# A decoder layer on one core: batch 0's mixture-of-experts stage sent through tiles of rows by expert, batch 1's kept dense

## The reference

```python
router_logits = x @ wg.T
probs = softmax(router_logits, axis=-1)
topk_w, topk_idx = top_k(probs, 2)
topk_w = topk_w / sum(topk_w, axis=-1, keepdims=True)
expert_w = sum(one_hot(topk_idx, 8) * topk_w[..., None], axis=1)
h1 = einsum('th,eih->tei', x, w1)      # i = 256 hidden units per expert
h3 = einsum('th,eih->tei', x, w3)
y = einsum('tei,ehi->teh', silu(h1) * h3, w2)
out = einsum('te,teh->th', expert_w, y)
```

## Time and profile before

| | us |
|---|---|
| median of 3 runs | 278.3 (276.68 to 278.51) |
| profiled execution | 279.73 |
| its span, first to last instruction | 278.0 |

### The profile page before, as it was taken

How to read it: one execution, slowest core, us unless ns; L and a number is a source line. 1 busy time by engine, 2 the same in 40 slices (tenths; PEclk the granted TensorE clock), 3 DMA queues, 4 the chain that set the end, 5 groups by cost and what they waited for, 6 DMA issues and landing times.

```text
span 278.0 us, 4261 instructions
## 1 busy us (share of the span) xinstructions
PE 256.4 (92%) x1294; PEld 158.6 (57%) x1294; DVE 189.1 (68%) x577; ACT 159.2 (57%) x298; POOL 121.4 (44%) x183
## 2 busy tenths in 40 slices
PE   7968899989998999999988989999999999999980
PEld 3345665766664755767643747457575565565630
DVE  5457878785999798466554698625989645545573
ACT  1568577776789767878686646684252423332300
POOL 9973191184332443325343420034562754554431
PEclk9968999999999999999999999999999999999995
DMA  7920000020001200000222000000000000000011
GB/s 250 343 81 1 2 0 1 2 63 15 2 0 39 112 4 4 0 0 4 75 75 75 2 1 0 2 1 0 2 0 0 1 2 0 0 0 0 2 38 38
DMA packets 5861, 8.62 MB, mean 31 GB/s; under 512 B 720, under 2 KB 3280, under 8 KB 5712
## 3 DMA queue, kind: packets, MB, share of 16 engines
q1 hardware_dynamic: 5264, 7.57, 8.6%
q10 hardware_dynamic: 576, 0.79, 0.9%
HBM read 7.83 MB, written 0.52 MB: 30 GB/s over the span
## 4 chain that ended last, share of the span: by engine, by line
PE 81%; ACT 8%; DVE 4%; issue 3%; DMA 1%; POOL 1%; POOLq 0%; DVEq 0%; ACTq 0%
PE psA L878 10%; PE psB L907 10%; PE psO L1016 10%; PE psO L930 9%; PE psB L785 4%; PE psJ L814 3%; PE psB L786 3%; PE psB L787 3%; PE psA L786 3%; PE psA L787 2%; PE psA L785 2%; ACT prob L1118 2%; PE psO L935 2%; PE psJ L891 2%; PE psJ L791 2%
## 5 line engine op out<-in xcount | busy, mean ns | idle before, releaser
L1298 DVE CUSTOM_DVE_ANT_0 junk<-psA,c 128x128 bf16<-128x128 f32 (+3 forms) x128 | 56.0, 487 | 15.0 <-PE psA L878 14.5
L756 POOL TENSOR_TENSOR gated<-silu,wbc 128x512 f32<-128x512 f32 x32 | 40.9, 1285 | 42.0 <-DVE hid L1414 21.9
L1118 ACT ACTIVATE prob<-psB 128x512 f32<-128x512 f32 (+1 forms) x88 | 47.5, 560 | 12.4 <-PE psB L907 10.5
L878 PE MATMUL psA<-kst,qa 128*128 128x512 f32 (+1 forms) x88 | 38.4, 451 | 3.3 <-ACT kst L1081 1.8
L907 PE MATMUL psB<-qb,kst 128*128 128x512 f32 (+3 forms) x128 | 38.7, 346 | 1.5 <-DVE kc L1240 0.6
L1172 ACT ACTIVATE silu<-psA 128x512 f32<-128x512 f32 x32 | 19.2, 600 | 35.5 <-PE psA L787 35.1
L1404 DVE SCALAR_TENSOR_TENSOR silu<-silu,psA 128x512 f32<-128x512 f32 x32 | 21.8, 682 | 19.7 <-ACT silu L1172 19.6
L1303 DVE TENSOR_REDUCE negm<-psA 128x3 f32<-128x462 f32 (+1 forms) x48 | 25.8, 579 | 13.0 <-PE psA L878 12.9
L1016 PE MATMUL psO<-hid,w 128*128 128x512 f32 x64 | 32.7, 593 | 0.0
L907 PEld LDWEIGHTS psB<-qb,kst 128*128 128x128 f32 x128 | 22.8, 188 | 16.4 <-issue 7.4
L741 POOL TENSOR_SCALAR_AFFINE_SELECT prob<-prob 128x256 f32<-128x256 f32 x32 | 13.0, 407 | 42.6 <-ACT prob_more L1118 42.6
(11 more groups left out here) (152 smaller groups left out, 504.5 us busy)
## 6 DMA issues: line engine op xcount, KB each, us to landing
c<-w_dram SPq DMA_DIRECT2D x8, 256.0 KB, 2.8
w<-w_dram SPq DMA_DIRECT2D x1, 1024.0 KB, 4.8
c<-c_dram SPq DMA_DIRECT2D x1, 666.0 KB, 7.8
xT<-xt_dram SPq DMA_DIRECT2D x2, 256.0 KB, 5.0
x_tok<-x_dram SPq DMA_DIRECT2D x1, 512.0 KB, 9.0
out_dram<-x_tok SPq DMA_DIRECT2D x2, 256.0 KB, 2.3
wx<-wx_dram SPq DMA_DIRECT2D x1, 384.0 KB, 7.1
c<-c_dram ACTq DMA_DIRECT2D x1, 320.0 KB, 6.4
```

What stands on the lines that cost most here:

```text
L756: nc.gpsimd.tensor_tensor(gated[:, n % 2, :], silu[:, n % 2, :], wbc[:, (E * b + f // 2) % 2, :], ALU.mult).then_inc(s_sg, 1)
L878: last = nc.tensor.matmul(ps[:, c:c + heads * width].rearrange("p (n w) -> p n w", n=heads), qa[:, u % SLOTS, 128 * i:128 * i + 128], keys ...
L1118: nc.scalar.activation(dst, psB[n % SIZE["B"]][:, 0:cols], ACT.Exp, scale=SCALE).then_inc(b_done[n % SIZE["B"]], 1)
L1298: last = nc.vector.tensor_tensor_reduce(out=junk[:, p, cols], in0=psA[p][:, cols], in1=c32[:, C_MASK + S - width:C_MASK + S], scale=-1.0, ...
```

## The change

Batch 0's dense expert stage (F1, F3, F2, BC, WT, YE and YT of batch 0) goes. Instead:

- `RT`: from the two expert numbers of each token VectorE marks choices; TensorE counts, with a triangular and an all-ones matrix, how many tokens before this one chose the same expert; VectorE turns ranks into places in a list in which every expert's tokens fill whole tiles of 128 rows, 15 tiles at most.
- `SX`: eight indexed transfers, issued by GpSimd, write 128 token rows each to their places in a buffer in device memory (`xs_d`). That buffer is zeroed at the start from a cleared key stack.
- `TE`: VectorE works out each tile's expert, and TensorE loads 15 numbers into registers.
- `XL` loads the rows back, four tiles at a time, issued by SyncE; `XS` transposes and splits them.
- `R1`, `R2`, `R3` for each of the 15 tiles: now the tokens are stationary and the weights move, addressed by register; silu and product on 256 hidden units; two transposes; two fp32 matmuls with w2.
- `YD` stores the results two tiles at a time; `YG` fetches them back to their tokens with eight indexed transfers; `YC` weights the two and adds the residual, on VectorE.

The row maxima's split (`MP`) of cross-attention moves from GpSimd to VectorE. The weights w1 and w3 share one buffer `wp`, so that one matmul moves 256 columns of each. Some buffers get other places. Cut to its core:

```diff
+NT = S * 2 // 128 + E - 1
+SEND = 1.2
-        add("MP", (u,), [("POOL", 0.55)], ...
+        add("MP", (u,), [("POOL", 0.55) if st == 0 else ("DVE", 0.4)], ...
+            add("RT", (), [("DVE", 0.55), ("PE", 0.6, 0), ("DVE", 1.7)], [("LG", (0,))])
+    for n in range(2 * QT):
+        add("SX", divmod(n, QT), [("POOL", SEND)], [("RT", ())], after=2.2)
+    add("TE", (), [("DVE", 0.5), ("PE", 1.5)], [("RT", ())])
+    for k in range(-(-NT // 4)):
+        add("XL", (k,), [("SP", 0.6)], [("SX", (1, QT - 1)), ("CQ2", (1,))] + ([(("XS", (k - 2,)), 0)] if k >= 2 else []), after=2.2)
+        add("XS", (k,), [("PE", 0.44), ("ACT", 0.5), ("DVE", 0.6)], [("XL", (k,))],
+            [(1, (("R1", (4 * k - 5,)), 0))] if k >= 2 else [])
+    for t in range(NT):
+        late = [(1, (("R1", (t - 2,)), 2)), (2, (("R2", (t - 2,)), 0))] if t >= 2 else []
+        add("R1", (t,), [("PE", 0.72), ("ACT", 0.32), ("DVE", 0.8)],
+            [("XS", (t // 4,)), ("TE", ()), ("WS", (2 * WC - 1,)), (("SQ", (1, 1, NG - 1)), 0)], late)
+        add("R2", (t,), [("PE", 0.24), ("ACT", 0.32)], [("R1", (t,))], [(1, (("R3", (t - 2,)), 0))] if t >= 2 else [])
+        add("R3", (t,), [("PE", 0.46), ("ACT", 0.22)], [("R2", (t,)), ("W2", ())], [(1, ("YD", (t // 2 - 2,)))] if t >= 4 else [])
+        if t % 2 or t == NT - 1:
+            add("YD", (t // 2,), [("SP", 0.6)], [("R3", (t,))], after=2.2)
+    for n in range(2 * QT):
+        add("YG", divmod(n, QT), [("POOL", SEND)], [("YD", ((NT - 1) // 2,)), last_pv(NU - 1)], after=2.2)
+    add("YC", (), [("DVE", 2.0)], [("YG", (1, QT - 1)), ("GATE", (0,)), ("LNX", (1, 1))])
...
+            sp.wait_ge(s_kz, SLOTS - 1)
+            sp.dma_start(xs_d.rearrange("(p n) d -> p (n d)", p=128),
+                         kst[:, SLOTS - 1, :, :].rearrange("p j t -> p (j t)")[:, 0:NT * D].bitcast(FP32)).then_inc(s_xz, 16)
...
+                    nc.gpsimd.indirect_dma_start(
+                        out=xs_d[:, :], out_offset=bass.IndirectOffsetOnAxis(ap=place_u[:, QT * k + i:QT * k + i + 1], axis=0),
+                        in_=x_tok[:, 0, i, :], in_offset=None).then_inc(s_sx, 16)
...
+                elif kind == "RT":
+                    nc.tensor.matmul(ps[:, 0:E * (QT + 1)], c16[:, H_TRI:H_TRI + 128], flat(chosen[:, :, :]), start=True, stop=False,
+                                     skip_group_check=True)
+                    for i in range(QT):
+                        rest_of = chosen[:, i:i + 1, :].to_broadcast([128, QT - i, E])
+                        last = nc.tensor.matmul(ps[:, E * (i + 1):E * (QT + 1)].rearrange("p (n e) -> p n e", e=E), c16[:, H_ONES:H_ONES + 128],
+                                                rest_of, start=False, stop=i == QT - 1, skip_group_check=True)
+                elif kind == "TE":
+                    pe.wait_ge(s_te, 1)
+                    for t in range(NT):
+                        expert_at.append(pe.value_load(tile_u[0:1, t:t + 1], min_val=0, max_val=I * (E - 1)))
+                elif kind == "R1":
+                    w = [wp[:, :, p, bass.ds(expert_at[t], I)] for p in range(PAIR)]
+                    nc.tensor.matmul(ps, xr_high[:, t % 8, :], w[0], start=True, stop=False)
+                    nc.tensor.matmul(ps, xr_low[:, t % 8, :], w[0], start=False, stop=False)
+                    nc.tensor.matmul(ps, xr_high[:, t % 8, :], w[1], start=False, stop=True).then_inc(s_a, 1)
+                elif kind == "R3":
+                    for n in range(2):
+                        at = I * (t % 2) + 128 * n
+                        last = nc.tensor.matmul(ps[:, 0:128], hT[:, at:at + 128], w2[:, bass.ds(expert_at[t] + 128 * n, 128)],
+                                                start=n == 0, stop=n == 1)
...
+                elif kind == "YC":
+                    for k in range(2):
+                        for i in range(QT):
+                            ins = nc.vector.scalar_tensor_tensor(out=z[:, i, :], in0=back[:, k, i, :], scalar=gsm[:, 0, 4 + k, i:i + 1],
+                                                                 in1=x_tok[:, 0, i, :] if k == 0 else z[:, i, :], op0=ALU.mult, op1=ALU.add)
```

More of the change, by code:

```diff
@@ L319, in schedule @@
             key = what if isinstance(what[0], tuple) else last(what)
-            extra = table[key[0]][2] if key == last(key[0]) else 0.0
+            extra = 0.0 if isinstance(what[0], tuple) else table[key[0]][2]
             before[item, n].append((key, LATENCY[table[key[0]][0][key[1]][0]] + extra))
@@ L484, in layer_kernel @@
         ot_sb = sb("ot_sb", [128, S])
-        junk = sb("junk", [128, SIZE["A"], S], BF16)
+        junk = shared("junk", [128, SIZE["A"], S], BF16)
+        choice = sb("choice", [128, 2, QT, E])
+        chosen = sb("chosen", [128, QT + 1, E], BF16)
+        over = sb("over", [128, E, E * QT])
+        first_tile = sb("first_tile", [128, E])
+        place = sb("place", [128, QT, E])
+        place_f = sb("place_f", [128, 2 * QT])
+        place_u = sb("place_u", [128, 2 * QT], U32)
+        before_t = sb("before_t", [1, 16, E - 1])
+        tile_f = sb("tile_f", [1, 16])
+        tile_u = sb("tile_u", [1, 16], U32)
+        sb("unused", [128, 232])
+        xs = rest
+        back = prob[:, 0, 0:2 * S].rearrange("p (k i d) -> p k i d", k=2, i=QT)
         z = sb("z", [128, QT, D])
@@ L561, in layer_kernel @@
         s_xh = sem("s_xh")
+        s_rt = sem("s_rt")
+        s_pl = sem("s_pl")
+        s_te = sem("s_te")
+        s_xz = sem("s_xz")
+        s_sx = sem("s_sx")
+        s_xl = [sem("s_xl0"), sem("s_xl1")]
+        s_rh = sem("s_rh")
+        s_rth = sem("s_rth")
+        s_ht = sem("s_ht")
+        s_yd = [sem("s_yd0"), sem("s_yd1")]
+        s_yg = sem("s_yg")
         s_sg = sem("s_sg")
@@ L603, in stack_free @@
                 eng.wait_ge(s_kz, u)
+                if u == SLOTS - 1:
+                    eng.wait_ge(s_xz, 16)
             else:
@@ L1242, in _ @@
                     free(JOB[item], last)
+                elif kind == "MP":
+                    u, = args
+                    p = u % 2
+                    fill_done(dve, "A", [("A", (u, k)) for k in range(len(a_fills(u)))])
+                    job_filled(dve, ("MT", (u - 2,)))
+                    rows = mpad[:, p, :, :].rearrange("q i (j c) -> q i j c", c=32)
+                    link(nc.vector.tensor_copy(rows[:, :, :, ROWS], negm[:, p, :, :]))
+                    nc.vector.tensor_tensor(rows[:, :, :, ROWS + 1], negm[:, p, :, :], rows[:, :, :, ROWS].bitcast(FP32),
+                                            ALU.subtract).then_inc(s_mp, 1)
                 elif kind == "VH":
@@ L1451, in constants @@
     c32[:, C_POW:C_POW + QT] = -0.5
+    first = np.full((E, E, QT), BIG, f)
+    for e in range(E):
+        first[e, :e] = 128 * np.arange(QT)
+    c32[:, C_THR:C_TAU] = first.reshape(-1)
+    c32[:, C_TAU:C_TAU + 16] = np.arange(16)
     c16 = np.zeros((128, NC16), f)
+    c16[:, H_TRI:H_TRI + 128] = np.arange(128)[:, None] < np.arange(128)
+    c16[:, H_ONES:H_ONES + 128] = 1
     c16[:, H_ID:H_ID + 128] = np.eye(128)
```

329 lines of the change are left out of this document (239 added, 90 removed), and 3 rows, old and new, of the table RINGS.

## The result

The changed kernel takes 282.9 us (median of 4 runs, 282.64 to 285.21) against 278.3 before (4 runs): a ratio of 1.020, 95% interval 1.013 to 1.026. It is slower, by 1.3 to 2.6%, where 275 and a gain of 1% had been forecast. The profiled execution has a span of 281.0 us, 3.0 more than before.

A forecast was written before the change was run, and what follows sets the result against it. TensorE was taken as the bound. First routed product at 195.5, plus 67.0 of TensorE work, 1.5 for VectorE, 2.3 for the clock, gives 266.3; with the 8.75 tail, span 275.0, forecast 275, range 266 to 286.

The forecast's parts named there:

- TensorE's relief of some 14 us: On TensorE 41 us of batch 0's dense work go; 25 us plus RT and TE come.
- The scatters: Eight on GpSimd from about 178, 1.2 us each, 9.6 in all, to 187.7; landed 190.0, rows loaded back 192.8.
- Rivals 1 and 2: Scatters slow at 2.3 us each, sum 283.8, chance 0.2; or cheap at 0.43 each, 269, chance 0.15.
- rival 1: Scatters at 2.3 instead of 1.2 us each: routed tiles start at 204.3, 284 on the median's scale; chance 0.2.
- TE at 1.5 us: Fifteen register loads on TensorE, at the planner's 1.5 us instead of 6.5 from the nearest row, an issue on a queue.
- Delay batch 1's chain by 5, which the routed tiles mostly cover: 276: Within rival 3: register loads at 6.5 us delay batch 1's chain by 5, mostly covered by routed tiles, time 276.
- Rival 3: Register-addressed matmuls or register loads cost TensorE: end 290 at 0.20 per matmul, 276 with loads at 6.5 us; chance 0.1.
- A tile of 1.56 us: TensorE time per routed tile: R1 0.89, R2 0.22, R3 0.45; 23.4 us for 15 tiles.
- TensorE near idle from 187 to 195, clock falling: Sign of being right: TensorE lacks filler before the routed tiles, 2 us of work in 9; half speed costs 2.3 us.
- Dense work of batch 1 from about 207: After batch 1's transposes near 197.5, router, gates and broadcast take 9.5 us, then its dense tiles begin.
- rival 4: Gathers in GpSimd's queue ahead of gate products make dense tiles wait: two or three 2 us stalls, about 279; chance 0.1.
- The return hidden: YD, gathers, YC and layernorm, 22 us, hidden behind batch 1's dense tiles if the last routed tile is done by about 250.

The follow-up runs named there:

- experiment 6: The kernel with one unchecked load, with every scatter issued twice, the second into a buffer nobody reads: 285.3 us.
- Experiment 4: The changed kernel with one load instruction for all fifteen registers and no bounds checks: 273.2 us, ratio 0.985 to the kernel before.
- experiment 9: One unchecked load, plus maxima split back on GpSimd, batch 0's last normalisation later on VectorE, or both: 272.6, 272.0 and 272.8 us.
- experiment 1: The changed kernel without register loads or register addresses, tile t fixed to expert t // 2: 271.8 us.

## Why the prediction was wrong, point by point

- **TensorE's relief of some 14 us:** right, 14.8.
- **The scatters:** right. The first issue came at 175.1 where 178 was forecast, the period is 1.27 where 1.2 was, so the last ended at 185.2 instead of 187.7, and the first rows were back at about 189.3 instead of 192.8. Rivals 1 and 2 are out; experiment 6 shows that rival 1's mechanism is real: rows that come 10.1 us later cost 12.7 us. The forecast had priced it at one for one (8.8 later, 8.8 longer), without the clock. That its total of 284 for 2.3 each is near the 285.3 measured for 2.5 a pair is luck: it was added to a sum 4 too high. (The terms given for the date of the first routed product add up to 195.0, not to 195.5; nothing hangs on that.) Experiment 4 had 0.6 us of spare, so the kernel stands right at that edge.
- **TE at 1.5 us:** wrong, 9.47 with its stop. This is the mis-sized term. The nearest row, the issue of 0.43, would have given 6.5, and even that is below what came. The number taken was the plan's, with no reason given. That the plan's other costs agree with rows, the ground given for its scatter price, would not have carried it: none of those rows was a register instruction.
- **The page's floor:** the floor of about 600 ns that the Trainium skill (DMA: Bandwidth & Descriptors, Latency and other measured facts) gives a `tensor_load` led to the prediction's estimate of 9 us for TE, and the stop of 9.47, 0.63 a load, is near that. The parts are others: 0.27 for each further load and 0.15 for each of its two checks. At the price so estimated the prediction still added only 1 us, which is the step below.
- **"Delay batch 1's chain by 5, which the routed tiles mostly cover: 276", and 1 us for all of TE at 9:** this step failed, and it did more harm than the size. The routed tiles couldn't cover anything. They stand in the same queue behind the loads, and they need the loaded numbers. The stop went into batch 1's attention, which is the chain that sets the end, and came out whole: 8.20 of 8.20, with 2.50 for the clock on top (the windows of experiment 4). With the 10.2 us by which the kernels with the dear and the cheap TE differ, the same forecast would have said 285. Rival 3 had the right cause at 0.1 and the wrong price.
- **Register-addressed matmuls:** R1 takes 0.49 + 0.23 + 0.25 in the chain (0.50 + 0.23 + 0.25 with fixed addresses), and the kernels with and without addresses differ by 0.7 us in all. The forecast of nothing was right.
- **A tile of 1.56 us:** about right (first R1 0.97, then two transposes 0.22 and R3 0.45), but the tiles of batch 1's waiting time come 1.9 us apart: 15 first products from 202.51 to 228.79. A tile above 1.8 us, and a first one after 202, were named as signs of being wrong, and both showed.
- **TensorE near idle from 187 to 195, clock falling:** it was idle earlier and longer, 178.06 to 187.53, and for another reason. Without the checked loads the forecast hole hardly existed: 8.39 of 9.14 us busy from 179.96 to 189.10 at a clock of 1.00. From 180 to 200 it was idle for 3.6 us there (8.48 and 7.95 busy in the two windows), not for the 8.5 us of filler that went, and the 2.3 us forecast for the clock were not lost. Against that, attention was to end near 186 and ended at 189.1. Why it didn't shorten by its filler is not settled; another plan (half the scatters, replanned) brought it to 187.2.
- **Dense work of batch 1 from about 207:** 224.9, and 214.75 with one unchecked load. From the transposes of batch 1 (L1081, 201.46) to the first dense product it took 13.3 us there, not 9.5. VectorE's routed products stand between the router's small operations, and TensorE's routed tiles ahead of the gates' transposes. But the 13 tiles done by then, against the six or seven that I had counted, made the rest shorter: 56.1 us behind the first dense product, where 275 - 207 = 68 was forecast. The sum of 275 without the stop was thus 4 too high (270.8).
- **The gathers (rival 4):** right to give it little. They fit between the gate products. Timeline of GpSimd, the kernel after:

```profile
240.44 1.29 POOL L868 TENSOR_TENSOR gated<-silu,wbc 128x512 f32<-128x512 f32 x1
241.90 0.99 POOL L859 DMA_INDIRECT prob<-ys_dram,place_u  x1 [0.16 <-DVE hid L1675]
242.90 1.31 POOL L868 TENSOR_TENSOR gated<-silu,wbc 128x512 f32<-128x512 f32 x1
```

- **The return hidden:** not quite. On VectorE the weighting of batch 0's rows stands ahead of batch 1's last products. Timeline of VectorE, then of TensorE, the kernel after:

```profile
260.34 2.21 DVE L1654 SCALAR_TENSOR_TENSOR z<-prob,gsm,x_tok 128x128 f32<-128x128 f32 x4
262.58 1.14 DVE L1654 SCALAR_TENSOR_TENSOR z<-prob,gsm,z 128x128 f32<-128x128 f32 x4
...
268.32 2.08 DVE L1548 TENSOR_SCALAR x_tok<-z,mv,rstd 128x128 f32<-128x128 f32 x4 [0.32 <-POOL rstd L877]
...
271.06 1.12 PE L1127 MATMUL psO<-hid,w 128*128 128x512 f32 x2 [0.92 <-DVE hid L1675]
```

  YC takes 3.35 us where 2 was forecast (beside a GpSimd product the four take 2.21, without 1.14, as in the earlier trace rows), and TensorE waits 1.5 us in two places for `hid`. This was missed.
- **The tail of 8.75:** right. The last F2 ends at 272.2, the span at 281.0: 8.8.
- **The move of MP at no cost:** right within what the runs can tell (experiment 9). On VectorE the last split holds `MT` up for 0.94 us (experiment 1), on GpSimd, behind a scatter, for 1.05.

## What to carry to other kernels

An instruction that computes nothing still holds its engine's queue. Price it with a row or a run of its own, and count the checks that a helper adds. Then ask what stands behind it in that queue: work behind a stop can't cover it. Here fifteen numbers loaded in the obvious way turned a change worth 1.5% into a loss of 2%; one load without checks, or loads placed in waits that exist, brought it back.

## What the runs showed of the hardware

- While TensorE's queue is at register loads from on-chip memory and their bounds checks, no matmul runs: 9.47, 5.66 and 1.27 us for 15 loads and 30 checks, one and 30, one and none. A further load costs 0.27 us and a check 0.15 us. The part that stays is not the same everywhere: the gap at one unchecked load was 0.56 to 1.40 us in other plans, and 15 loads with 30 checks took 8.56 in the kernel before. One load can fill fifteen registers.
- Matmuls with moving operands addressed by register run at the speed of fixed ones (0.49 + 0.23 + 0.25 us against 0.50 + 0.23 + 0.25 for the three of R1).
- In the stops of 9.47 and 8.56 us and behind them the granted clock was down (0.51 and 0.81 in two windows of 10 us, 0.75 and 0.74 for the second stop); after the first this cost another 2.5 us, a quarter on top of the stop. After the stop of 1.27 us it stayed at 1.00.
- Indexed writes of 128 rows of 512 bytes issue from GpSimd every 1.27 us, so without waiting for the one before, which takes about 2.2 us from issue to landing; the gathers took 0.99 us each of GpSimd's time between gate products.
